# Transposed rows kept in SBUF, expert weights loaded during attention, and a new order inside the attention step

## The reference, cut to what matters

```
xn = layernorm(x)
latent = xn @ latent_w + latent_b             # keys and values, 36 wide
q      = xn @ Wd_w[h] + Wd_b[h]               # 16 heads, 36 wide
attn   = softmax(causal(q @ latent.T) / sqrt(8));  z = attn @ latent
x = x + z @ out_w + out_b
      + gate * (relu(xn @ W1[e] + b1[e]) @ W2[e] + b2[e])     # e = argmax of xn @ Wr + br
```

## Time and profile before

| | us |
|---|---|
| median of 3 runs | 1721.79 |
| profiled execution | 1727.32 |
| its span, first to last instruction | 1725.6 |
| mean granted TensorE clock, as a share of 2.4 GHz | 0.949 |
| busy PE / PEld | 1505.9 / 1089.4 |
| busy DVE / ACT / POOL | 1159.3 / 1003.8 / 903.5 |

### The profile page before, as it was taken

One profiled execution on the slowest core, in us unless ns is written; L12 is line 12 of the kernel. 1 busy time (PEld: TensorE's weight loads), 2 busy tenths in 40 slices (PEclk: granted clock), 3 DMA queues, 4 the chain that ended last, 5 costly groups with the idle time before them and its releaser, 6 DMA issues.

```text
span 1725.6 us, 44847 instructions
## 1 busy us (share of the span) xinstructions
PE 1505.9 (87%) x13026; PEld 1089.4 (63%) x13027; DVE 1159.3 (67%) x4175; ACT 1003.8 (58%) x2526; POOL 903.5 (52%) x1625
## 2 busy tenths in 40 slices
PE   4799999999999999998995788888888888875883
PEld 4644555555555555547995677777777777764772
DVE  3357666666666666654553589998999999976661
ACT  3344555555555555553332788888888878852341
POOL 5324444444444444453445566666666666623663
PEclk9999999999999999999998799999999999996665
DMA  7403222222222222223331122112121121116444
GB/s 199 135 10 75 57 57 58 57 56 58 56 56 56 57 56 58 58 68 83 69 71 42 30 46 46 43 41 44 43 43 44 44 46 43 41 31 127 90 83 117
DMA packets 240883, 107.56 MB, mean 62 GB/s; under 512 B 145465, under 2 KB 229242, under 8 KB 240762
## 3 DMA queue, kind: packets, MB, share of 16 engines
q1 hardware_dynamic: 228410, 92.97, 22.4%
q0 software_dynamic: 10240, 13.64, 3.7%
q10 hardware_dynamic: 2176, 0.26, 0.1%
HBM read 61.92 MB, written 40.16 MB: 59 GB/s over the span
## 4 chain that ended last, share of the span: by engine, by line
PE 63%; ACT 16%; issue 6%; DVE 5%; POOL 5%; DMA 3%; SPq 1%; POOLq 0%; DVEq 0%; ACTq 0%
PE bankA L1831 8%; PE bankT L1854 8%; PE bankB L1877 7%; PE bankT L2028 4%; PE bankB L1893 3%; PE bankB L1884 3%; PE bankT L1863 3%; ACT qx L1613 3%; ACT km L1622 2%; ACT pe L1599 2%; ACT gqx L1613 2%; PE bankB L2091 2%; PE bankS L2017 2%; PE bankT L2017 2%; DVE pt L1308 2%
## 5 line engine op out<-in xcount | busy, mean ns | idle before, releaser
L949 DVE CUSTOM_DVE_ANT_0 masked<-bankS,causal 128x128 bf16<-128x128 f32 x512 | 128.6, 288 | 203.9 <-PE bankS L1844 203.0
L653 POOL TENSOR_SCALAR_AFFINE_SELECT probs<-probs 128x512 f32<-128x512 f32 x256 | 156.7, 635 | 160.6 <-ACT probs L1510 159.7
L1499 ACT ACTIVATE qT<-bankA,bd 128x256 f32<-128x256 f32 x256 | 107.3, 470 | 191.0 <-PE bankA L1831 186.8
L952 DVE CUSTOM_DVE_ANT_0 masked<-bankS,causal 128x256 bf16<-128x256 f32 x512 | 195.6, 419 | 0.2
L646 POOL CAST qb<-qT 128x256 bf16<-128x256 f32 x256 | 96.7, 398 | 130.0 <-ACT qT L1499 129.5
L1510 ACT ACTIVATE probs<-bankT 128x1024 f32<-128x1024 f32 x128 | 131.1, 1024 | 50.2 <-PE bankT L1854 50.2
L1831 PE MATMUL bankA<-xnT,wd 128*128 128x256 f32 x512 | 151.7, 421 | 0.0
L1854 PE MATMUL bankT<-qT,kT 37*128 37x512 f32 x512 | 146.3, 648 | 0.7 <-ACT probs L1510 0.7
L1877 PE MATMUL bankB<-probs,vaug 128*64 128x512 f32 x512 | 139.7, 624 | 0.9 <-ACT yT L1518 0.9
L1308 DVE STREAM_TRANSPOSE pt<-pe 128x768 f32<-128x768 f32 x128 | 124.4, 972 | 22.2 <-ACT pe L1599 21.8
L1518 ACT COPY yT<-bankB 128x512 f32<-128x512 f32 x128 | 75.0, 586 | 84.4 <-PE bankB L1884 84.4
(11 more groups left out here) (314 smaller groups left out, 4223.9 us busy)
## 6 DMA issues: line engine op xcount, KB each, us to landing
rzb<-reciprocals SPq DMA_DIRECT2D x128, 128.0 KB, 2.6
yT<-yT SPq DMA_DIRECT2D x64, 128.0 KB, 2.3
xtab<-tab SPq DMA_DIRECT2D x32, 192.0 KB, 2.0
xs_sorted<-zeros SPq DMA_DIRECT2D x1, 4608.0 KB, 18.7
qT<-xs_sorted SPq DMA_DIRECT2D x144, 32.0 KB, 1.7
ys_sorted<-qT SPq DMA_DIRECT2D x36, 128.0 KB, 1.9
value_rows<-vrow SPq DMA_DIRECT2D x32, 128.0 KB, 1.8
vx<-value_rows SPq DMA_DIRECT2D x256, 16.0 KB, 1.8
```

Source lines behind the costliest of these rows:

```text
L653: pool.affine_select(out=blocks, in_=blocks, compare_op=ALU.is_ge, fill=0.0, base=0, pattern=[[0, 4], [1, P]], channel_multiplier=-1).then ...
L949: dve.tensor_tensor_reduce(masked[:, e, 0:P], bankS[:, e, 0:P], causal[:, P:2 * P], -1.0, -NEG, ALU.add, ALU.min, mneg[:, n.half, e, j, 0:1])
L952: ins = dve.tensor_tensor_reduce(masked[:, e, P:3 * P], bankS[:, e, P:3 * P], causal[:, :], -1.0, -NEG, ALU.add, ALU.min, mneg[:, n.half, ...
```

## The change

- `xnT_all` keeps the transposed rows of all tokens (the chunks of the start are copied there and not to `xtmp`). GpSimd's `fetch` copies a batch's 256 columns from it to `xnT`. TensorE's `xnt`, ScalarE's copy behind it, `fetch_rows` and `xn` go.
- `xn_all` and `wall` share one place, `shelf`. The expert weights are loaded by SP in 12 calls (`experts(k)`, 16 transfers) in pairs 9 to 14 of the loop, after a wait for all scatters; the loop of SP ends at pair 9 (`CLEARED`) and the rest is written out. POOL and TensorE wait for them (`w_ex`) before the expert stage.
- Each batch from 2 to 17 scatters four tiles straight from `xn_all`, two before and two after `fetch`. The staging on VectorE goes.
- `layer1_masks` moves from the start into steps 0 and 1.
- TensorE's order in the step changes: the first `smax` and `qproj` come first, the two halves of `outp` stand around the second `smax`, `smax` 2, 3, 5 and 7 stand between the two parts of a score group, `qproj(m, 0)` takes the transposes' place, and `kv(m)` stands before the last values group.
- VectorE: `resid` comes after two reductions, one third of `normalise` after the last. The key evacuation signals by itself; the value evacuation has its own semaphore `va_sb`, and waits for the current batch's last values.

The core of the diff:

```diff
-        xn_all = sb("xn_all", [P, NT, C])
-        wall = sb("wall", [P, E0, WC])
+        shelf = sb("shelf", [P, E0 * WC])
+        wall = shelf[:, :].rearrange("p (e w) -> p e w", e=E0)
+        xn_all = shelf[:, 0:NT * C].rearrange("p (n c) -> p n c", c=C)
+        xnT_all = sb("xnT_all", [P, B * T])
@@ SP
+            for i in range(CLEARED, LOOP):
+                maxima(Batch(i + 1, 0))
+                denominators(Batch(i, 1))
+                if i == CLEARED:
+                    sp.wait_ge(S["scats"], 16 * NT)
+                experts(2 * (i - CLEARED))
+                maxima(Batch(i + 1, 1))
+                denominators(Batch(i + 1, 0))
+                experts(2 * (i - CLEARED) + 1)
@@ GpSimd
+            def fetch(m):
+                if type(m.pair) is int and m.pair == 0:
+                    pool.wait_ge(S["xt_act"], 1)
+                else:
+                    pool.wait_ge(S["q_ps"], (m.b - 1) * GROUPS)
+                passed(pool)
+                pool.tensor_copy(xnT[:, m.half, :], xnT_all[:, bass.ds(m.b * T, T)]).then_inc(S["xnT_sb"], 1)
@@ GpSimd, step(b, n, m, rows=None, groups=())
                 if n:
                     round_keys(n)
+                if rows is not None:
+                    scatter_rows(rows, rows + SCATTER // 2)
                 if n:
                     round_queries(n, 1)
+                if groups:
+                    pool.wait_ge(S["qb_sb"], n.b * PAIRS + 4)
+                for g in groups:
+                    layer1_masks(g)
+                if m:
+                    fetch(m)
+                if rows is not None:
+                    scatter_rows(rows + SCATTER // 2, rows + SCATTER)
                 clip(b, 0)
...
                 clip(b, 2)
-                clip(b, 3)
                 if m:
                     round_queries(m, 0)
+                clip(b, 3)
@@ VectorE
-                dve.tensor_scalar(kT[:, u, :], keys_ps[:, 0, 0:T], lb[:, 0:1], None, ALU.add)
+                dve.tensor_scalar(kT[:, u, :], keys_ps[:, 0, 0:T], lb[:, 0:1], None, ALU.add).then_inc(S["kv_sb"], 1)
+                if not (type(n.pair) is int and n.pair == 0):
+                    dve.wait_ge(S["av_done"], (n.b - 1) * GROUPS)
@@ VectorE, step(n, p, q): red 0, red 1, resid(q), red 2, invert(p), red 3, red 4, red 5,
@@   normalise(p, 0), red 6, normalise(p, 1), red 7, turn_maxima, normalise(p, 2)
@@ TensorE, step (before: outp both, smax 0, qproj 1, st 0, smax 1, qproj 2, st 1 around smax 2, av 0,
@@   smax 3, qproj 3, st 2 around smax 4, av 1, smax 5, xnt, st 3, smax 6, av 2, qproj(m, 0), smax 7, av 3, kv)
+   smax 0, qproj 1, outp(q, 0), smax 1, outp(q, 1), wait va_sb,
+   st 0 around smax 2, qproj 2, st 1 around smax 3, av 0,
+   smax 4, qproj 3, st 2 around smax 5, av 1,
+   smax 6, qproj(m, 0), st 3 around smax 7, av 2, kv(m), av 3
```

More of the change, by code:

```diff
@@ L681, in _ @@
             deviation0(1)
-            layer1_masks(0)
+            fetch(first)
+            fetch(second)
             deviation0(2)
@@ L695, in _ @@
             deviation0(7)
[L696 removed]
             round_queries(second, 0)
[L698 to L699 removed]
+            step(first, second, Batch(1, 0), None, (0, 1))
+            step(second, Batch(1, 0), Batch(1, 1), None, (2, 3))
             pool.wait_ge(S["xs_zero"], 16)
             pool.wait_ge(S["te_done"], 1)
[L702 to L706 removed]
+            for pair in range(1, CLEARED):
+                for b in (Batch(pair, 0), Batch(pair, 1)):
+                    step(b, b.next(), b.next().next(), (b.b - 2) * SCATTER)
+            with pool.Fori(CLEARED, LOOP) as i:
                 for b in (Batch(i, 0), Batch(i, 1)):
[L708 to L710 removed]
+                    step(b, b.next(), b.next().next())
+            step(Batch(LOOP, 0), Batch(LOOP, 1), None)
+            step(Batch(LOOP, 1), None, None)
             def first_weights(j, q, prior):
@@ L1073, in owners, with step @@
                 dve.tensor_scalar(te_i[:, :], tef[:, :], float(E0 - 1), None, ALU.min).then_inc(S["te_done"], 1)
-            def step(n, p, q, staged, prior=True):
-                if staged:
-                    stage(staged, prior)
+            def step(n, p, q):
+                if n:
+                    red(n, 0)
+                    red(n, 1)
                 if q:
@@ L1537, in _ @@
             chunk(0)
-            xnt(first)
             norm(1)
@@ L1557, in _ @@
             chunk(7)
-            xnt(second)
             maxima(first)
@@ L1838, in smax @@
                     pe.wait_ge(S["kb_sb"], n.b + 1)
+                    if type(n.pair) is int and n.pair == 0:
+                        pe.wait_ge(S["va_sb"], n.b + 1)
                 else:
@@ L1918, in step @@
                     qproj(n, 1)
+                if q:
+                    outp(q, 0, b.b * GROUPS)
+                if n:
+                    smax(n, 1)
+                if q:
+                    outp(q, 1, None)
+                if n:
+                    pe.wait_ge(S["va_sb"], n.b + 1)
                 st_first(b, 0, prior)
+                if n:
+                    smax(n, 2)
                 st_second(b, 0, prior)
                 if n:
-                    smax(n, 1)
                     qproj(n, 2)
@@ L1930, in step @@
                 if n:
[L1931 removed]
+                    smax(n, 4)
                     qproj(n, 3)
```

153 lines of the change are left out of this document (48 added, 105 removed).

## The result

The changed kernel takes 1733.2 us (median of 11 runs, 1724.8 to 1743.2), the kernel before 1720.8 on the same chip (11 runs, 1718.5 to 1725.9). The ratio is 1.0071, 95% interval 1.0045 to 1.0097: slower by about 12 us, where 1716.2 was forecast. The profiled executions differ by only 6.3 us, with spans of 1731.9 and 1725.6. That is because the profiled execution of the kernel before was a long one (1727.3, 6.5 us above the median of these eleven runs), while the changed kernel's lies at its median (1733.6). The runs of the changed kernel also spread over 18 us against 7, which is itself something to explain.

The account below looks back on a forecast made before the run. TensorE's own time was taken to bound steps 2 to 29. Gains of 7.8 us minus 0.8 (`kb`), 0.6 (start-up) and 0.8 (tail) gave 5.6 us, so 1716.2 us against a median of 1721.8; range 1708.5 to 1724.

Parts of the forecast that it names:

- The step of 21.12 us: Middle steps: 21.40 us minus 0.37 for the transposes plus 0.09 for the cut `outp`; 7.8 us gained in 28 steps.
- The new joints: TensorE's reordered matmuls in a step: other joints cancel, cutting `outp` by a `smax` costs 0.09 us, bounds 0 and 0.17.
- the 10.4 us: Rival for the loop steps: the cut of `outp` is free, steps gain 10.4 us, total 1710.7 us; chance 0.20.
- The thin handovers bite: Rival in the steps: `kb`, with 0.02 us margin, comes 0.25 us late each step; 1722 to 1723 us; chance 0.20.
- The bankB and reduction handovers: In a step: bankB's next user 1.43 us later, closest reductions 2.1 us apart; both at no cost.
- Three matter: The handovers judged critical in the new step: `kb` (0.8 us in all), bankB and the reductions (no cost).
- Scatters ... hidden: Four scatters a batch raise GpSimd from 10.6 to some 13 us a step, hidden behind the scores.
- Late denominators: Slower rival in the steps: scaling's denominators outrun a 1.2 us margin, 0.5 us a step; about 1730 us; chance 0.12.
- Start-up: Steps 0 and 1: loss of 0.6 us, bounds -3 to +2; step 2's first `smax` at 148.2 against 148.06.
- half of the old clock loss counted in: In the start-up estimate of -0.6 us, half of the old kernel's clock loss there was counted in.
- Expert weights: Loads moved into SP's free 7.5 us in four steps: taken as nothing, bounds 0 and 3 us in each.
- Tail: Step 30: `smax` 7 waits 0.6 us, last `av` and next `outp` some 0.8 each; 0.8 us lost.

Follow-up runs that it names:

- e4: Changed kernel with the first two scatters of a step moved behind the second and third clip; 1728.3 us, ratio 1.0035 to the kernel before.
- e3: Changed kernel with the last two scatters of a step moved behind the second and third clip; 1733.2 us, ratio 1.0060 to the kernel before.
- e1: Changed kernel with SyncE issuing all four transfers of a batch's maxima, ScalarE none; 1726.4 us, ratio 1.0016 to the kernel before.
- e5: Changed kernel with GpSimd waiting for the places only ahead of the first scatter, not before rounding keys; 1731.7 us, ratio 1.0050 to the kernel before.
- e6: Changed kernel with VectorE's gates and owners tables done between the later reductions of a step; 1731.4 us, ratio 1.0037 to the kernel before.
- e9: Changed kernel with the layer 1 masks made in the start-up as in the kernel before; 1731.4 us, ratio 1.0042 to the kernel before.
- e8: Changed kernel with the edits of e1, e5 and e6 together; 1718.6 us, ratio 0.9970 to the kernel before.
- e10: e8 with the layer 1 masks also made in the start-up; 1719.7 us, ratio 0.9973 to the kernel before.
- e7: Changed kernel with the edits of e4, e5 and e6 together; 1722.9 us, ratio 0.9995 to the kernel before.
- e2: Changed kernel without the scatters and the wait for them, so the experts read zeros; 1725.3 us, ratio 1.0023 to the kernel before.
- e12: e10 with VectorE's first inversion of denominators later and the scatters moved as in e4; 1727.1 us, ratio 1.0014 to the kernel before.

## Why the prediction was wrong

- **The step of 21.12 us: right.** 21.16 measured. The new joints cost 0.13 us (0.37 - 0.24) where I took 0.09 between 0 and 0.17. The trace now has the missing joint, in a step without scatters (TensorE; start us, us):

```profile
608.38 1.05 PE L1882 MATMUL bankB<-ow,yT 128*128 128x128 f32 x8
...
609.59 0.23 PE L1831 MATMUL bankS<-kb,qb 36*128 36x128 bf16 x2
...
609.86 1.16 PE L1882 MATMUL bankB<-ow,yT 128*128 128x128 f32 x8
...
611.17 1.13 PE L1843 MATMUL bankT<-qT,kT 37*128 37x512 f32 x4
```

  The halves of `outp` take 1.21 and 1.31 us from start to start, where the whole took 2.41: 0.11 for the cut. `kv`, now followed by values and not by `outp`, takes 1.00 instead of 0.90, and the `qproj` in front of `outp` 0.97 instead of 1.06. So the cut is not free, and the 10.4 us that came out by equal numbers of mode changes (the Trainium skill, TensorEngine Tiling (Array Packing), Key Properties) are not there.
- **"The thin handovers bite": did not come.** TensorE's matmuls do not wait for `kb` in the middle steps. The margin of 0.02 us was too small: in the step from 607 on, `kb` is ready at 606.86 and the `smax` starts at 607.14, while behind a real wait it starts 0.06 us after `kb` (152.21 to 152.27), so some 0.2 us are left. (The terms of the sum give 1.76 us, not 1.78, and VectorE idles 7.8 us in a step, not 8 or more; neither changes the forecast.) The bankB and reduction handovers held too.
- **"Three matter": the first step that failed.** I traced `kb`, bankB and the reductions, and the maxima only where I placed the expert loads: "the maxima, which `st` wants at 4.18 of the next step, against an issue that ends at 20.2". That is SyncE's half. ScalarE's half is issued at 0.1 to 1.2 of the next step, which leaves 2.9 us to land, and I never put it in the list. With scatters beside it that is too little by 0.3 to 0.9 us in twelve of thirteen steps. The old profile had both its issue, at 404.66, and, at the earlier trace rows, the copy that it stands behind.
- **"Scatters ... hidden": right for GpSimd's time, wrong as a whole.** I priced them on the engine that issues them and not for what they do to transfers already under way. The new order put the first one 0.2 us behind ScalarE's issue instead of 2.7; e4 takes that away and the waits go, e3 moves the other two away and they stay. The cost is 6.6 us by the profile (13 x (21.67 - 21.16)), of which 5.8 are seen as waits; e1 and e4 gain 9.5 and 6.2 us by the ratio.
- **Late denominators, the slower rival: wrong mechanism.** Near 1730 was its time and the result is near it, but that is chance: no normalisation waits for its denominators between 200 and 760 us, and the count of scatters, its ground, is not the cause.
- **Start-up: the second step that failed.** A loss of 0.6, at most 3, was forecast for steps 0 and 1 with the wait behind them, and together with the next three steps a gain of 0.2; they lost 7.2. The serialisation behind `te_done` was seen and put at a start near 148.2; the `smax` came at 152.27, since step 1 had already run to 149.75. Its wait for `kb` is 2.44 us. The masks' wait was put at 0.9 and is 2.4 to 2.5 at the full clock (2.48 in e5 and e6). The owners and gates were not in the sum at all: they stand on VectorE where `smax` 1 now comes early, and their waits are 1.56 and 0.57 us (200.95 and 178.06). The intervals say what removing each of them gives: 2.6 us for the keys (e5), 3.0 for the masks (e9 against e6), 1.5 for the owners (e6), 0.7 for the gates where the maxima are also in time (e8 against the changed kernel). That is 7.8 us, a little more than the 7.2 lost, as the kernel before had waits of its own there. With all of them removed (e10) batch 6 comes at 209.03 against 217.76, 8.7 us earlier, of which 1.3 lie before batch 2, where the clock rose earlier (four `qproj` take 1.13 us at 110.60, in the changed kernel 1.71 at 111.33).
- **The clock.** I had "half of the old clock loss counted in" as won back. In fact a fall is seen behind new waits: it cost 6.4 us in e1, and 4.3 in e8 (30.21 against e7's 25.92). That more waits make falls more frequent is likely, but not shown: how often the clock falls in each kernel is open, as an execution without a profile shows only its mean clock. So is what makes it fall in one execution and not in the next.
- **Expert weights: right.** They cost nothing: they are loaded between 554 and 787 us, and every interval from there to batch 31 is 21.16 us.
- **Tail: right.** It loses 0.8 as I said, by the waits that I named, 0.68 for the last `smax` against 0.6, and 0.69 and 0.78 ahead of `av` and `outp` against 0.8 each. That nothing was lost to the row loads holds too: the first `hidden` waits 0.92 us for VectorE in both kernels.
- **With the failed steps repaired the forecast comes out.** 1716.2 of 1721.8 us is a ratio of 0.9967; e8 and e10 measured 0.9970 and 0.9973.

## What to carry over

Put every transfer that a moved stage needs into the list of handovers, one line for each engine that issues a part of it: the last part to be issued sets the time, and it is queued behind whatever that engine waits for. A scatter is priced by what leaves beside it, not only by its issue. On TensorE, a wait of one to two microseconds in a thin start-up should be priced with the chance that the clock falls behind it, and short stretches with a low clock should be read again in an execution without one. Read the level of the clock from the lengths of like matmuls as well as from the granted clock: at the start of most profiles here the two do not agree.

## What was not expected of the hardware

- Where two scatters of 512-byte rows leave together with two 4 KB transfers of another queue, the scores wait 0.3 to 0.9 us for these (twelve waits in the changed kernel, thirteen in e3). With the scatters 3.2 us later nothing waits.
- The granted clock fell behind a single idle time of 1.56 us in e1 and not behind the same one in e2. TensorE had been busy without idle time from 176.2 to 197.4, where that wait begins; the clock came back to the full level by 213, with TensorE busy throughout since 199.
- The granted clock of the windows is 1.00 from 0 to 100 us in ten of the fourteen profiles, and yet TensorE runs at the lower level there: a group of four `qproj` matmuls takes 2.05 to 2.08 us where it starts between 33 and 103 us (in e4 up to 98), and 1.13 from 113 us on. In e5, e7, e9 and e12 the row gives 0.78 in the first 60 us and 0.50 from 60 to 100, and these are the ones that begin faster: the first `kv` part comes at 90.2 against 92.2 to 92.4. The router's 16 matmuls and the four behind them, in e10 and in e7:

```profile
29.84 3.42 PE L1802 MATMUL bankT<-lwr,xnT_all 128*128 128x8 f32 x16
33.12 2.05 PE L1825 MATMUL bankA<-xnT,wd 128*128 128x256 f32 x4
```
```profile
29.88 1.92 PE L1803 MATMUL bankT<-lwr,xnT_all 128*128 128x8 f32 x16
31.65 1.11 PE L1826 MATMUL bankA<-xnT,wd 128*128 128x256 f32 x4
```

  In e7 the clock is at the full level for these few us, and falls in the idle time behind them (granted 0.50 from 34 on). The next chunk starts at 37.27 instead of 39.23, and the 2 us last until the first `kv`. So TensorE is what the kernel waits for in this stretch, and a row of 1.00 there is not proof of the full clock. The mean clocks of these four executions are 0.929 to 0.935, those of the other ten 0.947 or more, which is how the two groups of executions in the section on the combinations were told apart. What makes the clock rise there in one execution and not in another is open.
